# Expert tiles of 256 rows with stationary weights for the first 50 slots of a routed feed-forward layer

## What is computed

```
x = x + attention(layernorm(x))                 # 16 heads of 64, causal
n = layernorm(x)
top_vals, top_idx = top_k(n @ Wr, 2)            # router: 2 of 8 experts for each token
rw = softmax(top_vals)
h  = silu(n @ Wg[e]) * (n @ Wu[e])              # 512 hidden units for each expert e
x  = x + sum over the two e of rw[e] * (h @ Wd[e]) / sqrt(12)
```

## Time and profile before

| | us |
|---|---|
| median of three runs | 909.01 |
| profiled execution | 901.64 |
| its span | 899.6 |
| PE busy (share) | 874.8 (97%) |
| DVE, ACT, POOL busy | 640.3, 617.3, 589.2 |
| first up product of slot 0 starts | 676.83 |
| first and last scatter of a slot start | 683.59 and 892.09 |

### The profile page before, as it was taken

How to read it: one execution, slowest core, us unless ns; L and a number is a source line. 1 busy time by engine, 2 the same in 40 slices (tenths; PEclk the granted TensorE clock), 3 DMA queues, 4 the chain that set the end, 5 groups by cost and what they waited for, 6 DMA issues and landing times. The chain is left out here.

```text
span 899.6 us, 20256 instructions
## 1 busy us (share of the span) xinstructions
PE 874.8 (97%) x6153; PEld 643.0 (71%) x6154; DVE 640.3 (71%) x2404; ACT 617.3 (69%) x1614; POOL 589.2 (65%) x598
## 2 busy tenths in 40 slices
PE   7999999999999999999999999999989999999995
PEld 3667667676767766777677767666657888888884
DVE  5677787878778787778777787888885664554542
ACT  4777777777777777777787787767785454445442
POOL 4385476578467748865795677576566677656664
PEclk9999999999999999999999999999999999999998
DMA  6495530000000000000000000000002333333332
GB/s 190 190 350 230 198 90 1 1 25 13 1 11 28 1 2 19 19 2 7 19 13 2 13 26 1 1 19 19 2 19 56 44 58 55 45 47 45 46 47 24
DMA packets 44006, 44.49 MB, mean 49 GB/s; under 512 B 4352, under 2 KB 35968, under 8 KB 43920
## 3 DMA queue, kind: packets, MB, share of 16 engines
q0 software_dynamic: 16528, 26.03, 12.0%
q1 hardware_dynamic: 27392, 17.39, 7.0%
HBM read 15.28 MB, written 28.12 MB: 48 GB/s over the span
## 5 line engine op out<-in xcount | busy, mean ns | idle before, releaser
L376 POOL TENSOR_TENSOR prob<-prob,row_inv 128x512 f32<-128x512 f32 (+3 forms) x256 | 319.3, 1266 | 213.1 <-DVE row_inv L713 213.0
L527 ACT ACTIVATE prob<-prob,neg_max 128x256 f32<-128x256 f32 (+3 forms) x512 | 280.5, 550 | 8.9 <-DVE neg_max L706 2.3
L1140 PE MATMUL low_ps<-PT,v_sb 128*64 128x512 f32 (+3 forms) x1024 | 152.0, 439 | 1.2 <-ACT PT L533 1.2
L1140 PEld LDWEIGHTS low_ps<-PT,v_sb 128*64 128x64 f32 x1024 | 68.1, 136 | 92.8 <-issue 60.4
L718 DVE COPY PT<-low_ps 128x512 f32<-128x512 f32 (+1 forms) x128 | 104.9, 819 | 35.5 <-PE low_ps L1127 33.6
L462 POOL DMA_INDIRECT out<-prob,meta_row x71 | 110.6, 1558 | 27.6 <-issue 26.4
L1127 PEld LDWEIGHTS low_ps<-ident,prob 128*128 128x128 f32 x640 | 74.5, 140 | 55.3 <-POOL prob L376 29.5
L538 ACT ACTIVATE v_sb<-mid_ps 128x512 f32<-128x512 f32 x64 | 38.2, 597 | 102.2 <-PE mid_ps L1070 102.0
L706 DVE CUSTOM_DVE_ANT_0 prob<-mid_ps,mask 128x128 f32<-128x128 f32 (+1 forms) x256 | 93.5, 421 | 5.6 <-PE top_ps L1113 0.2
L996 DVE TENSOR_TENSOR prob<-mid_ps,prob 128x512 f32<-128x512 f32 x71 | 49.1, 691 | 66.3 <-ACT prob L628 58.8
L527 ACT ACTIVATION_READ_ACCUMULATOR prob<-prob,neg_max 128x1 f32 x512 | 95.6, 187 | 0.0
(11 more groups left out here) (203 smaller groups left out, 1775.4 us busy)
## 6 DMA issues: line engine op xcount, KB each, us to landing
routed_rows<-W_dn POOLq DMA_DIRECT2D x8, 2080.0 KB, 7.9
qk_sb<-routed_rows SPq DMA_DIRECT2D x71, 65.0 KB, 1.9
X<-in_L_attn_x SPq DMA_DIRECT2D x8, 256.0 KB, 5.5
W_ffn<-in_L_ffn_Wg SPq DMA_DIRECT2D x8, 256.0 KB, 5.1
W_ffn<-in_L_ffn_Wu SPq DMA_DIRECT2D x8, 256.0 KB, 5.3
W_dn<-in_L_ffn_Wd SPq DMA_DIRECT2D x8, 256.0 KB, 4.5
out<-X SPq DMA_DIRECT2D x8, 256.0 KB, 2.3
out<-prob,meta_row POOLq DMA_INDIRECT x71, 3.3
```

Of the source, the lines that this page charges most:

```text
L376: nc.gpsimd.tensor_tensor(p_pair(i), p_pair(i), row_inv[:, i, :].unsqueeze(2).to_broadcast([P, 2, P * (i + 1)]), ALU.mult).then_inc(S["nor ...
L527: nc.scalar.activation(p_at(i, h), p_at(i, h), ACT.Exp, bias=neg_max[:, i, h:h + 1], scale=-1.0, accum_out=row_sum[:, i, h:h + 1]).then_in ...
L1140: last = nc.tensor.matmul(y_ps[h * HD:(h + 1) * HD, j * P:T], v_sb[:, half, j, o + h * HD:o + (h + 1) * HD], PT[:, h, j, j:NT, :].rearrang ...
```

## The change

Both kernels work through 71 slots with the same 8192 pairs. The change alters what the first 50 slots are, the table, the buffers and the start.

- **Wide tiles.** Slots 0 to 49 become 25 tiles of 256 rows of one expert (`WIDE`), two slots each. A slot of a wide tile is half of the expert's hidden units (256 of 512) for 256 rows. Now the weights are the stationary operand and the 256 transposed rows move: 12 products of 256 columns in place of 6 of 512. The hidden units then lie on partitions, so the four transposes of h and their copy go; the down product takes h as it is. Slots 50 to 70 stay tiles of 128 rows as before.
- **Half expert copies.** The stationary weights of a slot are in `half_up`, double buffered, where `qk_sb` was. For slots 4 to 49 ACT copies them, hi and lo, from `up_hi` and `up_lo` (`unit_copy`, two activations of 128x512). For slots 0 to 3 (`DIRECT`), ACT and DVE make them from the unsplit weights (`unit_hi`, `unit_lo`).
- **Three tables.** The first covers slots 0 to 31 with whole pairs of tiles among the rows of six batches, the second slots 32 to 49 with whole pairs among all rows (built in slots 12 to 17), the third slots 50 to 70 with what is left (slots 18 to 23). Each goes through the experts in ascending order.
- **Scatters.** They stay one for each 128 rows, 71 in all, with the same waits. The ring of result buffers has 8 places (`SPOTS`) in place of 4. The two results of a wide tile are ready together. Slots 1 and 3 no longer wait for the slot before.
- **Start.** The first tile is loaded and transposed in step 63 of attention; `unit_hi(0)`, `unit_lo(0)` and u of slot 0 come ahead of the last `values`, g of slot 0 after them. `split_lo(7)` moves into slot 2. The output of batch 7 is added after slot 1, not 0, and its statistics are taken after slot 2, not 1.
- **All slots are written out**; there is no loop.

With the counts above, the tables make these runs of one expert, in slots: 6, 6, 6, 6, 4, 4 (experts 0 to 5); then 2, 2, 2, 2, 2, 2 (experts 0 to 5), 6 (expert 6); then 1, 1, 1, 1, 1 (experts 0 to 4), 2 (expert 5), 3 (expert 6), 8 and 3 empty (expert 7).

```diff
+EARLY = 32
+WIDE = 25
+BROAD = 2 * WIDE
+SPOTS = 2 * RING
...
+            def scatter_slot(j):
+
+                q, spot = j % RING, j % SPOTS
+
+                last = S[f"eo_out{(j - 1) % RING}"]
+                seen(pool, S[f"eo_out{(j - 2) % RING}"], landings(j - 2))
+                if j >= RING:
+                    pool.wait_ge(last, nc.gpsimd.value_load(table[0:1, 2, bass.ds(j, 1)], min_val=16, max_val=16 * (SLOTS // RING + 1)))
+                elif j == 2:
                     pool.wait_ge(last, 16)
                 seen(pool, S["eo_done"], j + 1)
...
+            def unit_copy(j):
+
+                e = nc.scalar.snap(nc.scalar.value_load(table[0:1, 0, bass.ds(first_slot(tile_of(j)), 1)], min_val=0, max_val=E - 1))
+                if j == DIRECT:
+                    act.wait_ge(S["split_lo"], E)
+                seen(act, S["g_ready"], j - 1)
+                seen(act, S["u_ready"], j - 1)
+                for part in range(2):
+                    nc.scalar.activation(half_up[j % 2][:, part, :, :], up_halves[part][:, bass.ds(e, 1), j % 2, :, :].rearrange("p e b n -> p (e b) n"),
+                                         ACT.Copy).then_inc(S["unit_copied"], 1)
...
+            def tile_meta(t):
+
+                first, n = first_slot(t), len(slots_of(t))
+                spot, q = first % SPOTS, first % RING
+                seen(dve, S[f"x_tile_in{t % RING}"], landings(t))
+                for j in slots_of(t):
+                    seen(dve, S["gated"], j - SPOTS + 1)
+                    seen(dve, S[f"eo_out{j % RING}"], landings(j - SPOTS))
...
             def late(j):
 
-                if j == 0:
+                if j == 1:
                     post_x2(B - 1)
-                if j == 1:
+                if j == 2:
+                    split_lo(7)
                     post_stats(B - 1)
                     post_aggr(B - 1)
...
+            def tile_up(j, dst, part):
+
+                t = tile_of(j)
+                if t < WIDE:
+
+                    for c in range(2):
+                        last = passes(dst[:, c * PAIR:(c + 1) * PAIR],
+                                      [half_up[j % 2][:, a, part, c * P:(c + 1) * P] for a in range(2)],
+                                      [xT_tile[t % 2][:, a, :] for a in range(2)], True, True)
+                    return last
...
+            load_expert(0)
+            weights_in(0)
+            pe.wait_ge(S["x_lo"], 1)
+            tile_u(0)
+            values(STEPS - 1, NP - 1, False)
+            tile_g(0)
             project_out(STEPS - 1, NP - 1)
```

More of the change, by code:

```diff
@@ L53, in seen, with first_slot, tile_of, slots_of @@
         eng.wait_ge(sem, count)
[L56 to L62, removed]
+def first_slot(t):
+    return 2 * t if t < WIDE else t + WIDE
+def tile_of(j):
+    return j // 2 if j < BROAD else j - WIDE
+def slots_of(t):
+    return range(first_slot(t), first_slot(t + 1))
+def landings(j):
+    return 16 * (j // RING + 1) if j >= 0 else 0
 def layer(nc, x, w_down, w_up, w_q, w_out, Wr, Wg, Wu, Wd, out):
@@ L636, in turn @@
-            def turn(m, q, first=False, last=False, drain=False):
-                if not last and not drain:
-                    tile_xT(*after(m, q))
-                if not first:
-                    tile_hT(*before(m, q))
-                if not drain:
-                    tile_silu(m, q)
-            def late(j):
-                if j == 5:
-                    post_xn2T(B - 1)
-            tile_xT(0, 0)
-            post_out(B - 1)
-            for m in range(EARLY_TURNS):
-                for q in range(RING):
-                    turn(m, q, first=(m == 0 and q == 0))
-                    late(RING * m + q)
@@ L655, in _ @@
-            with act.Fori(EARLY_TURNS, TURNS) as m:
-                for q in range(RING):
-                    turn(m, q)
-            for q in range(LEFT):
-                turn(TURNS, q, last=(q == LEFT - 1))
-            turn(TURNS, LEFT, drain=True)
+            for j in range(SLOTS + 1):
+                turn(j)
+                late(j)
         @block.vector
@@ L757, in step @@
                     qk_lo(n + 1)
+                elif n == STEPS - 1:
+                    unit_lo(0)
+                    tile_xT(0)
                 if cur:
@@ L1006, in turn @@
[L1006 to L1014 removed]
+                seen(dve, S["down_ready"], min(j - 1, BROAD))
+                seen(dve, S["hT_ready"], j - 1 - BROAD)
+                nc.vector.tensor_tensor(h_sb[j % 2], u_ps[j % 2], silu_sb[j % 2], ALU.mult).then_inc(S["h_done"], 1)
@@ L1031, in late @@
                 if 12 <= j < 18:
-                    table_late(j - 12)
-            tile_xT(0, 0)
-            for m in range(EARLY_TURNS):
-                for q in range(RING):
-                    turn(m, q, first=(m == 0 and q == 0))
-                    late(RING * m + q)
-            with dve.Fori(EARLY_TURNS, TURNS) as m:
-                for q in range(RING):
-                    turn(m, q)
-            for q in range(LEFT):
-                turn(TURNS, q, last=(q == LEFT - 1))
-            turn(TURNS, LEFT, drain=True)
+                    table_late(j - 12, EARLY, BROAD)
+                if 18 <= j < 24:
+                    table_late(j - 18, BROAD, SLOTS)
+            for k in range(1, NP):
+                step(NP * (B - 1) + k, k, nxt=k < NP - 1, post=B - 2)
+            for e in (4, 2, 6):
+                split_lo(e)
+            unit_lo(1)
+            split_lo(3)
+            for j in range(SLOTS + 1):
+                turn(j)
+                late(j)
         @block.tensor
```

402 lines of the change are left out of this document (226 added, 176 removed).

## The result

| | before | after |
|---|---|---|
| median, us | 908.9 (907.94 to 910.8, 9 runs) | 915.75 (911.24 to 920.28, 9 runs) |
| ratio | 1 | 1.0073 (95%: 1.005 to 1.0097) |
| profiled execution, its span | 901.64, 899.6 | 915.37, 913.1 |

The changed kernel is slower by 6.9 us. The forecast was 911.8, the range 907.5 to 917.

What follows compares the result with a forecast made beforehand. POOL's scatters, waiting for landings, were taken to set the pace, with PE worth at most 8 us. Scatters +0.8 and start +2.0 made +2.8 us on a median of 909.0: 911.8 us, range 907.5 to 917.

Steps and rivals of the forecast that it cites:

- What bounds the kernel: Slots before the change: POOL's scatter steps, pace-setting from slot 28 on; a PE taking no time brings at most 8 us.
- The walk of 194 us: Kernel before, slot 1's scatter to slot 70's: about 194 us if only POOL's steps counted, against 201.93 measured.
- PE's wide slot: Slots 0 to 49 on PE: 2.53 us each instead of 2.88, worth 17.5 us if PE sets the end.
- ACT and DVE: Wide slots: ACT at most 2.24 us a slot, less than PE; DVE the same results; no cost.
- The scatters: Slots 1 to 70 on POOL: 202.7 us with 20 expert changes at 4.12 us each, +0.8 us against before.
- The start: Start of the slots: batch 7's statistics come later on DVE, so slot 1's scatter is 2.0 us later, 0 to 4.
- second rival: Start of the slots no later, only +0.8 us with small gains or losses: 908 to 910.5 us, chance 0.31.
- From the profiled execution to the median: Whole kernel: the median lies 7.4 us above the profiled execution; this difference was carried over to the forecast.
- PE setting the end: Rival, slots: landing waits cost less than said, so PE's savings count; about 887 us, chance 0.08.
- PE falling behind: Rival, wide slots: weight loads not hidden, 3.2 us a slot, or a clock fall; 922 us and above, chance 0.07.
- The start no later: Rival, start of the slots: slot 1's scatter not delayed, so 908 to 910.5 us; chance 0.31.
- Tables two and three: Slots 18 to 23 on DVE: six more steps, no cost, at most 2 us if POOL found a result late.

Runs made afterwards that it cites:

- after_pe: Changed kernel with three more identity transposes on PE in each of the 50 wide slots; 915.93 us, ratio 1.0066 to before.
- after_3: Changed kernel with up to three scatters in flight from slot 8 on; 901.75 us, ratio 0.9978 to before.
- after_nc: Changed kernel without scatter waits at a change of expert, results added to spare rows; 888.01 us, ratio 0.977 to before.
- nc kernels: Changed kernel and kernel before, both without scatter waits at a change of expert; 888.01 and 906.67 us on one chip.
- after_again: Changed kernel with no edit, measured and profiled a second time; 916.06 us, ratio 1.0082 to before.
- after_st: Changed kernel with batch 7's rstd and norm ahead of slot 0's scatter and its statistics one slot earlier; 908.37 us, ratio 1.0054 to before.
- before_again: Kernel before with no edit, run and profiled a second time; 909.92 us, ratio 1.0003 to before.
- w16: Changed kernel with 16 wide tiles instead of 25 and two tables instead of three; 900.58 us, ratio 0.9969 to before.
- w16_3: Changed kernel with 16 wide tiles, two tables and up to three scatters in flight; 895.56 us, ratio 0.9858 to before.
- before_3: Kernel before with up to three scatters in flight; 902.18 us, ratio 0.9983 to before.
- before_pe: Kernel before with two more identity transposes on PE in each slot; 917.69 us, ratio 1.011 to before.
- before_nc: Kernel before without scatter waits at a change of expert, results added to spare rows; 906.67 us, ratio 0.9971 to before.

## Why the prediction was right, and where its sizes were off

*What bounds the kernel.* Right for the change: the scatters decide after it (after_pe costs nothing, after_3 gains 8.6 us, after_nc 27.5). For the kernel before, the reading was half right. The text had PE hold POOL up by 8 us of 202 and spoke of POOL setting the pace from slot 28 on. The runs show that before, PE set the end: 15.6 us more of PE cost 10, and no waits at a change, or three scatters in flight, brought only 2.6 and 1.5. The walk of 194 us as what POOL alone would need fits both: POOL had room there, and PE's pace used it up.

*PE's wide slot*: forecast 2.53 us, measured 2.54 and 2.32 in turn. Its worth of 17.5 us is shown by the pair of nc kernels, 18.7, and none of it reached the time.

*ACT and DVE*: no cost, and none seen; the idle time added on DVE is waits for landings.

*The scatters*, +0.8 us, is the term that was sized too low. The walk was to be 202.7 and took 206.8, 209.0, 204.7 and 205.2 in the four kernels with the same slots (after, after_again, after_pe, after_st), while before's took 201.9 and 203.0: +1.7 to +7.1 in place of +0.8. The twenty changes cost 4.16 to 4.22 us on average in place of 4.12, 0.8 to 2.1 us more together: most of them 3.95 to 4.15, and one to five a run 4.5 to 5.1. The remaining 49 steps took 120.2 to 124.7 us, against 120.3. In after the long steps are those of slots 36 (5.12 us), 44 (5.14) and 64 (4.33, where no expert changes and 2.78 was taken). These three make 3.6 of the 4.1 us by which the walk exceeds the forecast, and slot 23 (below) makes 0.6. Slot 36's gate waited 2.85 us for the landing of slot 35's scatter, where its like at slot 34 waited 1.75:

```profile
795.95 0.18 POOL L484 TENSOR_TENSOR gate_p<-eps 128x1 f32<-128x1 f32 x1 [1.75 <-DMA out<-prob,meta_row]
...
798.59 1.56 POOL L486 DMA_INDIRECT out<-prob,meta_row  x1 [0.16 <-issue]
803.00 0.18 POOL L484 TENSOR_TENSOR gate_p<-eps 128x1 f32<-128x1 f32 x1 [2.85 <-DMA out<-prob,meta_row]
803.70 1.55 POOL L486 DMA_INDIRECT out<-y_sb,meta_row  x1 [0.53 <-issue]
```

DVE's `tile_meta` waited for the same landing, and PE behind it for 1.94 us. The first product after that finds the clock at half from 803.9 on, for 3.4 us, and the products behind it stand 0.20 to 0.22 us apart:

```profile
803.03 0.17 DVE L1061 COPY meta_w<-X 128x2 f32<-128x2 f32 x1 [3.17 <-DMA out<-prob,meta_row]
```

```profile
803.70 0.38 PE L1156 MATMUL top_ps<-xT_sb,qk_sb 128*128 128x256 f32 x1 [1.94 <-ACT qk_sb L655]
803.89 0.40 PE L1157 MATMUL top_ps<-xT_sb,qk_sb 128*128 128x256 f32 x1
```

So the late landing came first and the clock's fall after it; the fall is not what made the step long.

Why single landings come a microsecond or more later was not tested, but the traces name a neighbour that the prediction gave no price: the loading of instructions. Slots 28 to 67 were a loop before and are written out now. From slot 28's scatter to the last one the queues named `instruction` moved one packet before and fourteen after (window 774.17 to 892.09 of before, then 780.18 to 905.62 of after):

```profile
q14 instruction: 1, 0.01, 0.0%
```

```profile
q8 instruction: 7, 0.11, 0.4%
q14 instruction: 7, 0.06, 0.2%
```

By the semaphore updates, seven scatters of after land more than 3.9 us after their issue (slots 2, 26, 35, 36, 43, 47, 62). In six of them a packet of 16 KB on q8, 1.2 to 1.4 us long, starts 2.0 to 2.6 us after the issue; in slot 35 it is one of 8 KB on q14. Over all 13 traces, 41 of 104 scatters with such a 16 KB packet 0.9 to 3.2 us after their issue landed later than 3.9 us, and 8 of 802 without one. No kernel with a loop in its place was run, so this is a strong coincidence and not a shown cause. Late landings are in the traces of before as well (slot 28 of before_again waited for one, 5.16), but by the walk of 194 us the scatters had 8 us to spare there beside PE; after the change they have none. The walks named for after_3, w16 and w16_3 were too short by 4 to 7 us too; as the changed kernel's was, the differences between them came out all the same.

*The start*, +2.0 us. From `y_copy(63)` to slot 1's scatter it is, on one chip, 15.7 us with the start of before (before_3) and 16.3 with that of after (after_3, w16); on the second 16.5 (before_pe) and 17.4 (w16_3, after_again); on the third 16.6 (before_again, before_nc) and 18.2 and 18.7 (after_nc, after_pe). So it costs +0.6, +1.0 and +1.6 to 2.1: within the 0 to 4 given, and mostly below the value taken. Where attention was not disturbed it is 0.6, which is nearer to the second rival than to the forecast. The reason was right only in part. The order on DVE in after was as foreseen, and the statistics were done at 693.57:

```profile
690.50 0.60 DVE L1086 TENSOR_SCALAR prob<-low_ps,meta_w 128x128 f32<-128x128 f32 x2
...
691.16 1.22 DVE L933 TENSOR_TENSOR XT<-W_ffn,Wb 128x1024 fp32r<-128x1024 f32 x1
...
693.19 0.38 DVE L953 BATCH_NORM_AGGREGATE mv<-stats 128x2 f32<-128x6 f32 x4
```

But slot 0's scatter, which waits only for the result at 690.50, was itself at 691.77, and slot 1's comes 7.04 us after it in every kernel with this start, against 6.57 before. So 0.47 us are the statistics', for which POOL's rstd waits in between, and the rest is slot 0's own result, which in a wide tile comes from both halves' products: POOL stood idle for it 1.83 us in after and not at all in after_3. after_st, which took the statistics out of the way, did not bring slot 1 forward.

*From the profiled execution to the median.* Carrying over the 7.4 us came out right, by luck: the prediction gave no reason for it. They are the attention's, and belong to both kernels (before_again). The spans of before_again and after, 909.1 and 913.1, then differ by the start, +1.5 (18.1 less 16.6), the walk, +3.8 (206.8 less 203.0), and the attention, -1.3 (680.70 less 681.98): +4.0. The medians differ by 6.9, and in the repeat by 8.2. A walk of 209.0, as after_again had it, would make the first 6.2. How the walk is spread over executions was not measured beyond these traces.

The time came out 4 us above the forecast, inside the range. The mechanism was the forecast's, and the term that was too small is the scatters' +0.8: +4.1 more in the profiled walk, while the start's 2.0 was near the 1.5 of the pair above. The price of a change (4.12) held for most of the changes; what was left out are the late landings.

*The rivals.* PE setting the end (887): it is what after_nc shows (888.0), and what the landings forbid. PE falling behind: no, its slot takes at most 2.54 us where it waits for nothing. The clock's falls, which that rival named, came between slot 0 and the last ten slots at 694.7 and 803.9 us in after and at 722.1 in after_again (there for 6.8 us), at 872.8 in after_pe, and not at all in after_st. The walks of 206.8, 209.0, 204.7 and 205.2 us do not follow them: no long step of after_again stands at 722.1. The start no later: no, but by only 0.6 to 2.1 us.

*Tables two and three*: no cost is seen. Slot 23's step grew from 1.95 us to 2.55 (2.35 in after_again), but it is 2.54 in w16 as well, which builds no third table in slots 18 to 23. What makes it longer stays open.

## What to carry to other kernels

When a matmul change moves which work follows which, count what it does to the waits of the transfers behind it: here the same rows in 25 wide tiles changed expert 20 times in place of 12, and with the waits at these changes 18 us of PE came to nothing. To find which of two engines near balance sets the end, compare the start of the last product with the start of the last store, or add work to one of them; a stretch in which an engine reads 100% busy can be an engine that runs ahead. Once PE and the scatters were both eased (16 wide tiles, 13 changes, three scatters in flight) the kernel came 1.4% under the one before. When a loop is written out, look at what the instruction queues move beside the transfers that you wait for.

## What the runs showed of the hardware

- One attention phase, instruction for instruction the same, ended at 674.4 to 683.0 us after the start of the span. The difference grows in holes of about 1 us on DVE ahead of one form of the mask instruction (idle 5.6 against 14.8 us in all). On one chip four traces lay between 674.4 and 676.2, on another four between 680.9 and 683.0.
- An indirect transfer with addition of 128 rows of 512 B lands 3.2 to 3.3 us after its issue in the usual case. Single ones take more, up to 3.8 in the view of before and 5.0 in after_3:

```profile
DMA to landing us min/median/max: 3.2/3.3/5.0
```

- Most of the late ones have a 16 KB packet of an `instruction` queue beside them: 41 of the 49 landings over 3.9 us in the 13 traces.
- Falls of the granted clock to half came up to three times ahead of the last slots in a run (22.2, 694.7 and 803.9 us in after, each over by 3.4 us later; one of 6.8 us in after_again), and none in the first profile of before. At half clock the products of 256 columns stand 0.21 us apart in place of 0.12.
